# Node one-hots as the stationary operand, edge products of two groups in two halves of the array, and x in node order

## The chip, the cores and the metric

The kernel runs on one core of a Trainium2 chip. The metric is the device time of one execution in microseconds. The engines are PE (TensorE, matmul), DVE (VectorE), ACT (ScalarE), POOL (GpSimd) and SP (SyncE, which here only starts transfers); each works through its own list of instructions in order and waits on semaphores for the others.

## The reference

A graph network layer over 3125 nodes of 128 features and 53125 edges (sorted by destination, with self loops), each edge with 64 features of its own:

```
h   = relu(bn1(concat(x[src], edge_attr) @ W1 + b1))     # 53125 x 128
agg = segment_sum(h, dst) / max(count(dst), 1)           # 3125 x 128
h2  = relu(bn2(concat(x, agg) @ W2 + b2))                # 3125 x 256
z   = relu(h2 @ Wl + bl)
out = layernorm(x + z)
```

`bn` normalises each column over all rows, so bn1 needs the sum and the sum of squares of every column over all edges before any edge can be normalised.

## The kernel before

**Stages.** The product of x with the upper 128 rows of W1 is made once for each node, as a table `ytab` in DRAM, so that an edge needs one row of the table plus the product of its 64 features with the lower 64 rows of W1. The edge stage (to about 466 us) makes h for all edges, keeps it in SBUF (each fourth group goes to DRAM) and sums h and its square. A second pass (475 to 570 us) normalises, and sums h over windows of destinations; the node stage follows it. The change touches the edge stage alone, and the loads ahead of it.

**The edge stage.** There are 26 cycles (`NI`); a cycle i has four groups q = 0 to 3 (`U`), a group has four tiles of 128 edges, so 512 edges. I write (i, q) for a group. For each group:

- POOL gathers the table rows, one indirect transfer for each tile of 128 edges (`gather`, L672 to L688). The gathers of a group wait until h of the group four before it is ready (L676).
- PE multiplies the edge features with W1 (`product`, L762): an instruction takes two tiles, whose features stand in partitions 0 to 63 and 64 to 127, against a block-diagonal `w1e` of 128 x 256. The result is in PSUM bank `psP[q]`, one bank for each q.
- DVE adds the two (`make_h`, L1282) and counts up `h_ready`; adds h to a running sum (`sum_h`, L1335); ACT squares h (`squares`, L1019), and DVE adds the square to another running sum (`sum_sq`, L1342), one group late: `sum_sq` of (i, q-1) stands behind `sum_h` of (i, q).

**Rows that PE fetches.** In cycles 2 to 22 (`NODES`) one group (`NODEQ`, q = 2) has its first two tiles (even i) or three tiles (odd i) not gathered but made on PE (`node_tiles`, L55). DVE compares the source number of each edge with the node numbers (`node_onehots`, L1300), five batches for a cycle, each for 5 of 25 node tiles, in a ring of three buffers (`RING`). PE multiplies the table, kept in SBUF as three bfloat16 parts (`exact`), with the one-hots (`node_batch`, L774): the table part is stationary, the one-hots move, 256 or 384 columns at a time, 75 matmuls in a cycle. The result stands in `noderows` (feature by edge) and has to be turned: ACT copies it to SBUF (`rows_out`, L1097), and PE multiplies it with the identity into `psP[2]` (`rows_back`, L793).

**The counts and the product of x.** Once in a cycle DVE makes one-hots of the destinations (`onehots`, L1271), PE sums them (`counts`, L834) and ACT copies four rows of the result (`place_counts`, L1041). In 14 cycles PE also makes a piece of x @ W2 for the node stage (`x_product`, L845), reading the turned x of the table stage with a stride; ACT copies it (`x_product_out`, L1031) and saves it. `counts` and `x_product` share a PSUM bank and take turns through `cnt_placed` and `x_out`.

**Orders.** PE's order in a cycle is `edge_step` at L852: node batches 0 and 1, `x_product`, product (i, 2), node batch 2, product (i, 3), node batches 3 and 4, product (i+1, 0), `counts`, product (i, 1), `rows_back`. DVE's is `edge_step` at L1354: per group `make_h`, `sum_h`, `sum_sq`, and behind (i, 0) node one-hots 0 and 1 of the next cycle, behind (i, 1) the destinations' one-hots and node one-hots 2, behind (i, 2) node one-hots 3 and 4. ACT's is the loop at L1106: `rows_out`, the square of (i, 0), the store of the one-hots, `place_counts` (which waits for `counts` of the same cycle), the square of (i, 1), then `x_product_out` (for i below 14), then `node_numbers` of cycle i+2 (L1071), then the squares of (i, 2) and (i, 3). SP's is the loop at L526: store the fourth group, load edge features three cycles ahead, load source numbers.

Of the kernel before, what the change touches and what calls it, by code (L numbers as in the profile page):

```python
# [33 lines left out]
P = 128  # L34
# [4 lines left out]
U = 4  # L39
# [8 lines left out]
NODEQ = 2  # L48
# [6 lines left out]
def node_tiles(i):  # L55

    return 2 + i % 2 if ROWS0 <= i < ROWS1 else 0


def gnn_kernel(nc, E, x, xt, src, src_rows, dst, dst_rows, ea, W1, b1, g1, be1, W2, b2, g2, be2, Wl, bl, out):  # L60
# [29 lines left out]
    with ctx:  # L90
# [6 lines left out]
        def sem(name):  # L97
            return ctx.enter_context(nc.semaphore(name))
# [25 lines left out]
        w1e = sb("w1e", [P, 2, F])  # L124
        iota = sb("iota", [P, WIN])
        nodeid = sb("nodeid", [P, NT])[:, :]
        rowst_sb = sb("node_rows_turned", [P, MOST * P])
# [86 lines left out]
        XSTEPS = [(h, k, min(XP, PN - k)) for k in range(0, PN, XP) for h in range(H2)]  # L214
        w2x = agg[:, 0:H2 * P]
# [8 lines left out]
        assert XW <= 512 and len(XSTEPS) <= XT0 // (KEEP * GF) - 1  # L224
# [10 lines left out]
        noderows = psP[1][:, 0:MOST * P]  # L235
# [12 lines left out]
        PRODUCTS = [(0, q) for q in range(U)] + [(1, 0)]  # L248
        for i in range(1, NI):
            order = [(i, 1), (i, 2), (i, 3)] + ([(i + 1, 0)] if i + 1 < NI else [])  # L250
            PRODUCTS += order if i not in NODES else order[1:] + order[:1]

        def products_through(i, q):

            return PRODUCTS.index((i, q)) + 1

# [9 lines left out]
        s_w = sem("w_loaded")  # L266
# [12 lines left out]
        rows_kept = sem("node_rows_turned_copied")  # L279
        rows_added = sem("node_rows_added")  # L280
# [12 lines left out]
        s_tab = sem("table_written")  # L293
        x_ps = sem("w2_x_psum")
# [177 lines left out]
        def _(sp):  # L472
# [6 lines left out]
            sp.wait_ge(s_w, 1)  # L479
            sp.dma_start(w1e[0:FE, 0, :], W1[F:F + FE, :]).then_inc(s_cols, 16)  # L480
            sp.dma_start(w1e[FE:P, 1, :], W1[F:F + FE, :]).then_inc(s_cols, 16)
# [40 lines left out]

            load_ea(1, 1)
            load_nodes_of(ROWS0)
            load_ea(2, 0)
            for i in range(NI - 3):  # L526
                spill_out(i, i % 2)
                load_ea(i + 3, (i + 1) % 2)
                if i + 3 in NODES:
                    load_nodes_of(i + 3)  # L530
            spill_out(NI - 3, 1)
# [115 lines left out]
        def _(pool):  # L647
# [24 lines left out]
            def gather(i, q):  # L672

                g = U * i + q
                if g >= U:
                    pool.wait_ge(h_ready, g - 3)  # L676
                if i >= 2 and q == KEEP:
                    pool.wait_ge(spilled[i % 2], 16 * (i // 2))
                if (i + 1) * KEEP * GF > XT0 and q == 0:
                    pool.wait_ge(x_ps, len(XSTEPS))  # L680
# [54 lines left out]
        def _(pe):  # L735
# [26 lines left out]
            def product(i, par, nth, q):  # L762
                g = U * i + q
                if q == 0:
                    pe.wait_ge(ea_loaded[par], 16 * nth)
                pe.wait_ge(h_ready, g - U + 1)
                more = q == NODEQ and i in NODES
                for b in range(2):
                    last = pe.matmul(psP[q][:, b * 2 * F:(b + 1) * 2 * F], ea_cols(par, q, b),  # L769
                                     w1e[:, :, :].rearrange("p a f -> p (a f)"), start=(b == 0 or not more),  # L770
                                     stop=not more)
                last.then_inc(prod_ready, 1)

            def node_batch(i, b):  # L774

                t0, t1 = NODECUT[b]
                w = node_tiles(i) * P
                if (i, b) == (ROWS0, 0):
                    pe.wait_ge(consts_kept, 2)
                    pe.wait_ge(second_parts, len(PIECES))  # L780
                    pe.wait_ge(third_parts, len(PIECES))
                if b == 0:
                    pe.wait_ge(h_ready, U * (i - 1) + 2)
                pe.wait_ge(nhot_ready, batch_index(i, b) + 1)
                hots = node_chunks(i, b)
                for t in range(t0, t1):
                    for k in range(PARTS):
                        last = pe.matmul(noderows[:, 0:w], exact[k][0:PN, t * F:(t + 1) * F],  # L788
                                         hots[:, (t - t0) * w:(t - t0 + 1) * w], start=(t == 0 and k == 0),
                                         stop=(t == NT - 1 and k == PARTS - 1))  # L790
                last.then_inc(nhot_used, 1)

            def rows_back(i):  # L793

                pe.wait_ge(rows_kept, i - ROWS0 + 1)
                for j in range(node_tiles(i)):
                    last = pe.matmul(psP[NODEQ][:, j * F:(j + 1) * F], rowst_sb[:, j * P:(j + 1) * P], ident[:, :],
                                     start=False, stop=(j == node_tiles(i) - 1))
                last.then_inc(rows_added, 1)

            def ea_cols(par, q, b):

                at = (q * 2 + b) * P
                return eat[par][:, at:at + P]
# [12 lines left out]
            def product_first(q):  # L817
# [6 lines left out]
                for b in range(2):  # L824
                    last = pe.matmul(psP[q][:, b * 2 * F:(b + 1) * 2 * F], ea_cols(0, q, b),
                                     w1e[:, :, :].rearrange("p a f -> p (a f)"), start=(b == 0), stop=(q >= EARLY and b == 1))
# [18 lines left out]
            def x_product(m):  # L845

                h, k, n = XSTEPS[m]
                pe.wait_ge(cnt_placed, m + 1)
                pe.matmul(psT[1][:, 0:n * NT].rearrange("o (p t) -> o p t", t=NT), w2x[:, h * P:(h + 1) * P],  # L849
                          xtv[:, :, k:k + n].rearrange("f t p -> f p t"), start=True, stop=True).then_inc(x_ps, 1)  # L850

            def edge_step(i, par, nth):  # L852
                node = i in NODES
                if node:
                    node_batch(i, 0)
                    node_batch(i, 1)
                else:
                    product(i, par, nth, 1)
                if i <= len(XSTEPS):
                    x_product(i - 1)  # L860
                product(i, par, nth, 2)
                if node:
                    node_batch(i, 2)
                product(i, par, nth, 3)
                if node:
                    node_batch(i, 3)
                    node_batch(i, 4)
                if i + 1 < NI:
                    product(i + 1, 1 - par, (i + 1) // 2 + 1, 0)
                counts(i, par)  # L870
                if node:
                    pe.wait_ge(rows_kept, i - ROWS0 + 1)
                    product(i, par, nth, 1)
                    rows_back(i)
# [7 lines left out]
            product(1, 1, 1, 0)  # L882
# [119 lines left out]
        def _(act):  # L1002
# [94 lines left out]
            def rows_out(i):  # L1097

                w = node_tiles(i) * P
                act.wait_ge(nhot_used, NB5 * (i - ROWS0 + 1))  # L1100
                if i > ROWS0:
                    act.wait_ge(rows_added, i - ROWS0)
                act.activation(rowst_sb[:, 0:w], noderows[:, 0:w], ACT.Copy).then_inc(rows_kept, 1)  # L1103

            x_product_out(0)
            for i in range(1, NI - 1):  # L1106
                if i in NODES:
                    rows_out(i)
# [111 lines left out]
        def _(dve):  # L1220
# [8 lines left out]
            dve.memset(w1e[:, :, :], 0.0).then_inc(s_w, 1)  # L1229
# [15 lines left out]
            for a in range(2):  # L1245
                last = dve.tensor_tensor(w1e[:, a, :], w1e[:, a, :], sgn, ALU.mult)
            last.then_inc(s_wsgn, 1)
# [34 lines left out]
            def make_h(i, par, nth, q):  # L1282
# [9 lines left out]
                if q == NODEQ and i in NODES:  # L1292
                    w = node_tiles(i) * F
                    dve.wait_ge(rows_added, i - ROWS0 + 1)
# [59 lines left out]
            def edge_step(i, par, nth):  # L1354
                for q in range(U):
# [11 lines left out]
                    if q == 0:  # L1367
                        node_onehots(i + 1, 0)
                        node_onehots(i + 1, 1)
                    if q == 1:  # L1370
                        onehots(i + 1)
                        node_onehots(i + 1, 2)
                    if q == 2:
                        node_onehots(i + 1, 3)
                        node_onehots(i + 1, 4)
# [253 lines left out]
```

## Time and profile before

| | |
|---|---|
| median of 3 runs | 611.88 us (611.45 to 613.88) |
| profiled execution | 613.19 us, span of its instructions 611.4 us |
| busy in the span | PE 523.2 us (86%), PE weight loads 402.0, DVE 453.0 (74%), ACT 212.9, POOL 387.9 (63%) |
| mean granted PE clock | 0.934 of 2.4 GHz |
| edge stage, last gather begins | 465.51 us |
| second pass | 475 to 570 us |

The busy time of POOL counts the writing of a gather's descriptors and not the gap to the next one. Matmuls are pipelined: a record lasts longer than the spacing of two records, and the time of "xN" records in one row includes the last one's tail. A float32 matmul shows as two records, each with a weight load.

### The profile page before, as it was taken

What the parts mean: (1) busy time and instruction counts of PE and PEld (TensorE: products, weight loads), DVE (VectorE), ACT (ScalarE), POOL (GpSimd) and SP (SyncE); (2) the same over time, 40 slices, a digit from 0 to 9 for tenths busy, and PEclk for the clock granted to TensorE, in tenths of its full rate; (3) what the DMA queues carried; (4) which work ended last, traced back from release to release, by engine and by line L of the source; (5) the groups of instructions that cost most, each with busy time, mean ns of one, the idle gap of its engine ahead of it and who ended that gap; (6) DMA issues with size and microseconds to landing.
All of it is one profiled execution on the core that took longest, in us unless ns stands there. A gap on an engine that the chain in (4) does not pass through costs nothing.

```text
span 611.4 us, 11185 instructions
## 1 busy us (share of the span) xinstructions
PE 523.2 (86%) x3396; PEld 402.0 (66%) x3396; DVE 453.0 (74%) x747; ACT 212.9 (35%) x568; POOL 387.9 (63%) x487
## 2 busy tenths in 40 slices
PE   4639999999999999999897989854448999999983
PEld 4527666766757677777666676632225999999573
DVE  4598878686888868797877788654435877777786
ACT  2253222232313232222222221221116456666466
POOL 4777777777777777777777777777773233333500
PEclk9778999999999999999999999975568899999998
DMA  7635434443435444444444243442232478777004
GB/s 193 229 112 172 144 119 145 149 152 106 152 125 153 147 142 133 134 130 134 130 129 139 86 140 107 126 129 94 86 103 87 131 229 229 232 233 220 13 1 105
DMA packets 49561, 84.38 MB, mean 138 GB/s; under 512 B 11490, under 2 KB 25682, under 8 KB 49521
## 3 DMA queue, kind: packets, MB, share of 16 engines
q1 hardware_dynamic: 31420, 49.21, 25.3%
q0 software_dynamic: 11648, 23.88, 15.0%
q10 hardware_dynamic: 6453, 10.79, 5.1%
q8 instruction: 21, 0.34, 0.2%
q14 instruction: 19, 0.16, 0.1%
HBM read 63.74 MB, written 20.08 MB: 137 GB/s over the span
## 4 chain that ended last, share of the span: by engine, by line
POOL 41%; PE 27%; issue 17%; DVE 8%; DMA 4%; ACT 2%; ACTq 0%; POOLq 0%; DVEq 0%
POOL res L685 29%; POOL work L685 11%; PE psH L929 8%; PE psC L929 8%; PE psH L788 5%; DMA res<-ytab,srci 1%; PE psT L849 1%; DVE res L1481 1%; POOL res L667 1%; DMA srci<-in_src 1%; PE psH L769 1%; DMA res<-in_x,srci 1%; DVE res L1312 1%; ACT res L1068 1%; PE psT L769 1%
## 5 line engine op out<-in xcount | busy, mean ns | idle before, releaser
L685 POOL DMA_INDIRECT res<-ytab,srci x248 | 237.3, 957 | 75.6 <-issue 73.1
L788 PE MATMUL psH<-res 125*128 125x256 bf16 (+1 forms) x1575 | 222.5, 298 | 9.6 <-DVE res L1298 8.6
L788 PEld LDWEIGHTS psH<-res 125*128 125x128 bf16 x1575 | 152.3, 98 | 72.9 <-DVE res L1298 13.4
L685 POOL DMA_INDIRECT work<-ytab,srci x104 | 98.3, 946 | 31.7 <-issue 31.4
L1312 DVE TENSOR_TENSOR res<-agg,psC 125x1280 bf16<-125x1280 bf16 (+1 forms) x105 | 99.1, 971 | 4.9 <-PE psH L788 4.8
L1298 DVE TENSOR_TENSOR res<-psH,res 128x512 f32<-128x512 f32 x50 | 34.5, 689 | 80.3 <-DMA res<-ytab,srci 42.1
L1449 DVE TENSOR_TENSOR work<-res,psX 128x512 f32<-128x512 f32 x103 | 69.7, 687 | 21.0 <-PE psC L929 15.8
L710 POOL TENSOR_TENSOR agg<-agg,srci 128x64 f32 x104 | 32.3, 311 | 72.0 <-ACT srci L1163 58.5
L1345 DVE TENSOR_TENSOR psX<-agg,psX 128x512 f32<-128x512 f32 x103 | 71.1, 690 | 2.5 <-ACT agg L1023 2.4
L769 PE MATMUL psH<-w1e,work 128*128 128x256 f32 x200 | 55.6, 403 | 11.7 <-DVE res L1298 11.7
L1023 ACT ACTIVATE agg<-res 128x512 f32<-128x512 f32 x78 | 48.7, 624 | 46.7 <-DVE res L1298 28.8
L1338 DVE TENSOR_TENSOR psS<-res,psS 128x512 f32<-128x512 f32 x78 | 54.3, 696 | 2.7
L929 PE MATMUL psH<-work 128*128 128x128 f32 (+1 forms) x416 | 51.7, 278 | 1.0 <-DVE work L1449 1.0
L929 PE MATMUL psC<-work 128*128 128x128 f32 (+1 forms) x416 | 51.4, 277 | 0.0
L929 PEld LDWEIGHTS psH<-work 128*128 128x128 f32 x416 | 49.4, 195 | 1.2 <-DVE work L1449 1.2
L929 PEld LDWEIGHTS psC<-work 128*128 128x128 f32 x416 | 49.3, 195 | 0.0
L769 PEld LDWEIGHTS psH<-w1e,work 128*128 128x128 f32 x200 | 36.7, 201 | 18.8 <-issue 10.0
L1103 ACT ACTIVATE node_rows_turned<-psH 128x256 f32<-128x256 f32 (+1 forms) x21 | 9.1, 435 | 102.2 <-PE psH L788 102.2
L769 PEld LDWEIGHTS psT<-w1e,work 128*128 128x128 f32 x100 | 20.7, 216 | 32.4 <-issue 13.6
L769 PE MATMUL psC<-w1e,work 128*128 128x256 f32 x100 | 30.4, 431 | 11.6 <-DVE work L1298 11.6
L769 PE MATMUL psT<-w1e,work 128*128 128x256 f32 x100 | 30.4, 431 | 9.7 <-DVE res L1298 5.9
L1051 ACT ACTIVATE cnt<-psT 1x64 f32 x104 | 22.5, 216 | 36.4 <-PE psT L841 33.1
(204 smaller groups left out, 549.8 us busy)
## 6 DMA issues: line engine op xcount, KB each, us to landing
work<-in_edge_attr SPq DMA_DIRECT2D x26, 512.0 KB, 3.6
spill<-work SPq DMA_DIRECT2D x26, 256.0 KB, 2.4
res<-spill SPq DMA_DIRECT2D x25, 256.0 KB, 3.2
res<-ytab,srci POOLq DMA_INDIRECT x248, 2.5
hot_dram<-hotb ACTq DMA_DIRECT2D x13, 256.0 KB
hot_dram<-work ACTq DMA_DIRECT2D x13, 256.0 KB
hotb<-hot_dram SPq DMA_DIRECT2D x13, 256.0 KB, 2.7
work<-hot_dram SPq DMA_DIRECT2D x13, 256.0 KB, 2.9
```

What stands on the lines that cost most here:

```text
L685: pool.indirect_dma_start(rows[:, j * F:(j + 1) * F], None, ytab, bass.IndirectOffsetOnAxis(ap=srci[:, j, g:g + 1], axis=0)).then_inc(gath ...
L710: pool.tensor_tensor(w, w, wsum[:, q, :], ALU.add).then_inc(agg_added, 1)
L769: last = pe.matmul(psP[q][:, b * 2 * F:(b + 1) * 2 * F], ea_cols(par, q, b), w1e[:, :, :].rearrange("p a f -> p (a f)"), start=(b == 0 or ...
L788: last = pe.matmul(noderows[:, 0:w], exact[k][0:PN, t * F:(t + 1) * F], hots[:, (t - t0) * w:(t - t0 + 1) * w], start=(t == 0 and k == 0), ...
L929: last = pe.matmul(psA[q][:, 0:n], mx[:, q, j * F:(j + 1) * F], hotf[:, q, j * WIN:j * WIN + n], start=(j == 0), stop=(j == TILES - 1))
L1023: act.activation(sq[g % 2], slot(i, i % 2, q), ACT.Square).then_inc(sq_ready, 1)
L1051: last = act.activation(cnt[r:r + 1, bass.ds(bases[q], WIN)], psT[1][r:r + 1, q * WIN:(q + 1) * WIN], ACT.Copy)
L1298: dve.tensor_tensor(h, psP[q][:, :], h, ALU.add).then_inc(h_ready, 1)
L1312: dve.tensor_tensor(node_chunks(i, b).rearrange("p (t e two) -> p t e two", t=t1 - t0, two=2), srcz[i % 2][0:PN, 0:w].rearrange("p (e two) ...
L1338: last = dve.tensor_tensor(psS[:, :], slot(i, par, q), psS[:, :], ALU.add)
L1345: last = dve.tensor_tensor(psX[:, :], sq[g % 2], psX[:, :], ALU.add)
L1449: dve.tensor_tensor(tiles(mx[:, q, :]), tiles(hin), negu, ALU.max).then_inc(m_ready, 1)
```

## The change

- `NODEQ` is 3, and PE makes three tiles in each of cycles 2 to 22 (63 tiles; before 52).
- In `node_batch` the one-hots are stationary (128 edges) and the table parts move (128 columns): 3 x 25 x 3 = 225 matmuls of 128 columns in a cycle, which add directly into `psP[3]` on top of the edge product. `rows_out`, `rows_back`, `noderows` and their semaphores go.
- The edge products run in pairs of groups (`two_products`): even groups have their features in partitions 0 to 63, odd ones in 64 to 127, and matmuls of 64 rows by 128 columns alternate between the two halves. `w1e` is 128 x 128 (the same weights twice), and the features are laid out accordingly. A pair waits for h of its second bank's last user, and `make_h` of either group waits for both.
- `x_product` reads x from a transposed input in node order, loaded by SP in 7 chunks, two products to a chunk.
- PE's and DVE's orders change; ACT's order is as before, without `rows_out`.

```
 NODEQ = 3;  node_tiles(i): 3 in cycles 2 to 22
             def ea_product(par, q, j, start, stop):
                 half = slice(q % 2 * FE, (q % 2 + 1) * FE)
                 at = (q // 2 * TILES + j) * P
                 return pe.matmul(psP[q][:, j * F:(j + 1) * F], eat[par][half, at:at + P], w1e[half, :], start=start,
                                  stop=stop)
             def two_products(i, par, nth, q):
                 if q == 0:
                     pe.wait_ge(ea_loaded[par], 16 * nth)
                 pe.wait_ge(h_ready, U * (i - 1) + q + 2)
                 for j in range(TILES):
                     for k in (q, q + 1):
                         ...
                         last = ea_product(par, k, j, j == 0 or not more, not more)
# node_batch
                 for t in range(t0, t1):
-                    for k in range(PARTS):
-                        last = pe.matmul(noderows[:, 0:w], exact[k][0:PN, t * F:(t + 1) * F],
-                                         hots[:, (t - t0) * w:(t - t0 + 1) * w], ...)
+                    for j in range(node_tiles(i)):
+                        at = (t - t0) * w + j * P
+                        for k in range(PARTS):
+                            last = pe.matmul(psP[NODEQ][:, j * F:(j + 1) * F], hots[:, at:at + P],
+                                             exact[k][0:PN, t * F:(t + 1) * F], start=False, ...)
# x_product
                 pe.wait_ge(cnt_placed, m + 1)
+                pe.wait_ge(x_chunk, 16 * (m // H2 + 1))
-                pe.matmul(psT[1][...], w2x[:, h * P:(h + 1) * P], xtv[:, :, k:k + n].rearrange("f t p -> f p t"), ...)
+                pe.matmul(psT[1][:, 0:n * NT], w2x[:, h * P:(h + 1) * P], xchunk[:, 0:n * NT], start=True, stop=True)
# PE, one cycle
             def edge_step(i, par, nth):
+                two_products(i, par, nth, 2)
                 if node:
                     node_batch(i, 0)
                     node_batch(i, 1)
-                else:
-                    product(i, par, nth, 1)
                 if i <= len(XSTEPS):
                     x_product(i - 1)
-                product(i, par, nth, 2) ... product(i, par, nth, 3) ...
                 if node:
+                    for b in range(2, NB5):
+                        node_batch(i, b)
                 if i + 1 < NI:
+                    two_products(i + 1, 1 - par, (i + 1) // 2 + 1, 0)
                 counts(i, par)
-                if node: ... product(i, par, nth, 1); rows_back(i)
# DVE, make_h of the group that PE fetches
-                    dve.wait_ge(rows_added, i - ROWS0 + 1)
+                    dve.wait_ge(nhot_used, NB5 * (i - ROWS0 + 1))
# DVE, behind make_h, sum_h, sum_sq of group q of cycle i
                     if q == 0:
+                        node_onehots(i, 3)
+                    if q == 1:
+                        node_onehots(i, 4)
+                        onehots(i + 1)
+                    if q == 2:
                         node_onehots(i + 1, 0)
                         node_onehots(i + 1, 1)
+                    if q == 3:
+                        node_onehots(i + 1, 2)
# SP, in the loop of a cycle
+                if i % 2 and i // 2 + 1 < len(XCHUNKS):
+                    load_x_chunk(i // 2 + 1)        # waits for x_ps, then 128 x 500 float32
# ACT
             for i in range(1, NI - 1):
-                if i in NODES:
-                    rows_out(i)
                 squares(i, 0)
                 hot_out(i, i % 2)
                 place_counts(i)
                 squares(i, 1)
                 ...
```

## Rows read from the trace of the kernel before

**Rows 1.** The chain that ended last, by line (share of the span).

```profile
by line: POOL res L685 29.1%; issue 16.7%; POOL work L685 10.8%; PE psH L929 7.8%; PE psC L929 7.7%; PE psH L788 4.7%; DMA res<-ytab,srci 1.3%; PE psT L849 1.3%; DVE res L1481 1.1%; POOL res L667 1.1%; DMA srci<-in_src 1.0%; PE psH L769 1.0
```

**Rows 2.** One stretch: length; busy PE, PEld, DVE, ACT, POOL; PEclk; DMA share; GB/s.

```profile
105.00:404.00 299.00, 282.12 (x1794) 202.10 (x1792) 236.64 (x337) 79.33 (x189) 226.16 (x240) 1.00 0.44 132
```

**Rows 3.** Timeline of POOL: start, length, what, idle before.

```profile
421.77 0.94 POOL L685 DMA_INDIRECT work<-ytab,srci  x1 [0.30 <-issue]
...
465.51 0.94 POOL L685 DMA_INDIRECT work<-ytab,srci  x1 [0.30 <-issue]
```

**Rows 4.** Timeline of PE: node batches, product, counts and rows_back.

```profile
260.91 3.44 PE L788 MATMUL psH<-res 125*128 125x256 bf16 x30
...
266.35 0.61 PE L797 MATMUL psT<-ident,node_rows_turned 128*128 128x128 f32 x4
...
276.49 5.04 PE L788 MATMUL psH<-res 125*128 125x384 bf16 x30
281.37 1.03 PE L769 MATMUL psH<-w1e,work 128*128 128x256 f32 x4
282.23 0.60 PE L841 MATMUL psT<-work,onesb 128*128 128x256 bf16 x4
...
283.54 0.83 PE L797 MATMUL psT<-ident,node_rows_turned 128*128 128x128 f32 x6
```

**Rows 5.** Groups by form: busy us, mean ns of one, idle before.

```profile
L788 PEld LDWEIGHTS psH<-res 125*128 125x128 bf16 x1575 | 152.3, 98 | 72.9 <-DVE res L1298 13.4
...
L1312 DVE TENSOR_TENSOR res<-agg,psC 125x1920 bf16<-125x1920 bf16 x50 | 55.6, 1146 | 0.0
...
L849 PE MATMUL psT<-res,agg 128*128 128x500 f32 x24 | 24.7, 1119 | 10.0 <-ACT cnt L1051 10.0
```

**Rows 6.** Timeline of DVE: the fetched group of three tiles, sums, node one-hots.

```profile
255.76 0.28 DVE L1295 TENSOR_TENSOR res<-psT,res 128x128 f32<-128x128 f32 x1
255.96 0.54 DVE L1296 COPY res<-psT 128x384 f32<-128x384 f32 x1
...
272.06 0.69 DVE L1345 TENSOR_TENSOR psX<-agg,psX 128x512 f32<-128x512 f32 x1
272.66 2.21 DVE L1312 TENSOR_TENSOR res<-agg,psC 125x1920 bf16<-125x1920 bf16 x2
...
278.35 0.69 DVE L1298 TENSOR_TENSOR res<-psH,res 128x512 f32<-128x512 f32 x1 [1.55 <-DMA res<-ytab,srci]
...
280.28 1.54 DVE L1312 TENSOR_TENSOR res<-agg,psC 125x1280 bf16<-125x1280 bf16 x2
```

**Rows 7.** Timeline of ACT: the copies of the counts and the square behind them.

```profile
266.50 0.90 ACT L1051 ACTIVATE cnt<-psT 1x64 f32 x4 [1.22 <-PE psT L841]
267.43 0.63 ACT L1023 ACTIVATE agg<-res 128x512 f32<-128x512 f32 x1
```

**Rows 8.** Timelines of DVE, PE and ACT around the product of x in cycle 2.

```profile
54.27 2.04 PE L849 MATMUL psT<-res,agg 128*128 128x500 f32 x2
...
55.92 0.69 DVE L1298 TENSOR_TENSOR work<-psC,work 128x512 f32<-128x512 f32 x1 [0.62 <-DMA work<-ytab,srci]
...
56.35 0.59 ACT L1037 ACTIVATE agg<-psT 128x500 f32<-128x500 f32 x1 [3.52 <-PE psT L849]
...
58.53 0.69 DVE L1345 TENSOR_TENSOR psX<-agg,psX 128x512 f32<-128x512 f32 x1 [1.19 <-ACT agg L1023]
```

**Rows 9.** Timeline of PE behind two idle times, and the granted clock of the first.

```profile
44.45 2.22 PE L849 MATMUL psT<-res,agg 128*128 128x500 f32 x2 [9.99 <-ACT cnt L1051]
...
48.17 1.69 PE L769 MATMUL psC<-w1e,work 128*128 128x256 f32 x4
49.70 1.03 PE L769 MATMUL psH<-w1e,work 128*128 128x256 f32 x4
...
404.74 2.07 PE L769 MATMUL psT<-w1e,work 128*128 128x256 f32 x4 [2.20 <-DVE res L1296]
...
40.00:49.00 9.00, 4.55 (x8) 2.79 (x9) 8.74 (x16) 4.86 (x11) 6.82 (x7) 0.50 0.41 132
```

More of the change, by code:

```diff
@@ L47 @@
 ROWS1 = 23
-NODEQ = 2
+NODEQ = 3
 MOST = 3
@@ L55, in node_tiles, with gnn_kernel @@
 def node_tiles(i):
-    return 2 + i % 2 if ROWS0 <= i < ROWS1 else 0
-def gnn_kernel(nc, E, x, xt, src, src_rows, dst, dst_rows, ea, W1, b1, g1, be1, W2, b2, g2, be2, Wl, bl, out):
+    if not ROWS0 <= i < ROWS1:
+        return 0
+    return 3
+def gnn_kernel(nc, E, x, xt, xcols, src, src_rows, dst, dst_rows, ea, W1, b1, g1, be1, W2, b2, g2, be2, Wl, bl, out):
     N, F = x.shape
@@ L214, in gnn_kernel @@
         XSTEPS = [(h, k, min(XP, PN - k)) for k in range(0, PN, XP) for h in range(H2)]
+        XCHUNKS = [(k, n) for h, k, n in XSTEPS if h == 0]
         w2x = agg[:, 0:H2 * P]
@@ L223, in gnn_kernel @@
         assert SQ0 >= NAGG // 2 and SQ0 + 2 * GF <= NAGG - MOST * P
-        assert XW <= 512 and len(XSTEPS) <= XT0 // (KEEP * GF) - 1
+        xchunk = agg[:, SQ0 - GF:SQ0 - GF + XW]
+        assert Z0 + MOST * P <= SQ0 - GF
+        assert XW <= 512
         psT = [pb(f"psT{i}", [P, 512]) for i in range(2)]
@@ L246, in node_chunks @@
             return ring[batch_index(i, b) % RING][0:PN, 0:(t1 - t0) * node_tiles(i) * P]
[L248 to L251, printed above, removed]
+        PRODUCTS = [(0, q) for q in range(U)] + [(i, q) for i in range(1, NI) for q in range(U)]
         def products_through(i, q):
-            return PRODUCTS.index((i, q)) + 1
+            return PRODUCTS.index((i, q | 1 if i else q)) + 1
         negu = psX[:, 0:F].unsqueeze(1).broadcast_to([P, TILES, F])
@@ L265, in gnn_kernel @@
         s_w1x = sem("w1x_loaded")
-        s_w = sem("w_loaded")
         s_rows = sem("dst_loaded")
@@ L293, in gnn_kernel @@
         s_tab = sem("table_written")
+        x_chunk = sem("x_chunk_loaded")
         x_ps = sem("w2_x_psum")
@@ L478, in _ @@
                              ).then_inc(s_x[k], 16)
-            sp.wait_ge(s_w, 1)
-            sp.dma_start(w1e[0:FE, 0, :], W1[F:F + FE, :]).then_inc(s_cols, 16)
-            sp.dma_start(w1e[FE:P, 1, :], W1[F:F + FE, :]).then_inc(s_cols, 16)
+            for a in range(2):
+                sp.dma_start(w1e[a * FE:(a + 1) * FE, :], W1[F:F + FE, :]).then_inc(s_cols, 16)
             sp.dma_start(w2x, W2[0:F, :]).then_inc(s_cols, 16)
@@ L521, in load_nodes_of, with load_x_chunk @@
                              ).then_inc(s_srcb, 16)
+            def load_x_chunk(m):
+                k, n = XCHUNKS[m]
+                if m == 0:
+                    sp.wait_ge(prod_ready, EARLY)
+                else:
+                    sp.wait_ge(x_ps, H2 * m)
+                sp.dma_start(xchunk[:, 0:n * NT], xcols[:, k * NT:(k + n) * NT]).then_inc(x_chunk, 16)
             load_ea(1, 1)
             load_nodes_of(ROWS0)
+            load_x_chunk(0)
             load_ea(2, 0)
@@ L530, in _ @@
                     load_nodes_of(i + 3)
+                if i % 2 and i // 2 + 1 < len(XCHUNKS):
+                    load_x_chunk(i // 2 + 1)
             spill_out(NI - 3, 1)
@@ L760, in _ @@
             pe.wait_ge(s_wsgn, 2)
-            def product(i, par, nth, q):
-                g = U * i + q
+            def ea_product(par, q, j, start, stop):
[4 more added lines that the diff above has]
+            def two_products(i, par, nth, q):
                 if q == 0:
                     pe.wait_ge(ea_loaded[par], 16 * nth)
[L766 to L772, printed above, removed]
+                pe.wait_ge(h_ready, U * (i - 1) + q + 2)
+                for j in range(TILES):
+                    for k in (q, q + 1):
+                        more = k == NODEQ and i in NODES
+                        last = ea_product(par, k, j, j == 0 or not more, not more)
+                        if j == TILES - 1:
+                            last.then_inc(prod_ready, 1)
             def node_batch(i, b):
@@ L786, in node_batch @@
                 for t in range(t0, t1):
[L787 to L790, printed above, removed]
-                last.then_inc(nhot_used, 1)
[L793 to L804, printed above, removed]
+                    for j in range(node_tiles(i)):
+                        at = (t - t0) * w + j * P
+                        for k in range(PARTS):
+                            last = pe.matmul(psP[NODEQ][:, j * F:(j + 1) * F], hots[:, at:at + P],
+                                             exact[k][0:PN, t * F:(t + 1) * F], start=False,
+                                             stop=(t == NT - 1 and j == node_tiles(i) - 1 and k == PARTS - 1))
+                last.then_inc(nhot_used, 1)
             def turn_first(q):
@@ L823, in product_first @@
                     pe.wait_ge(s_idx, 1)
-                for b in range(2):
-                    last = pe.matmul(psP[q][:, b * 2 * F:(b + 1) * 2 * F], ea_cols(0, q, b),
-                                     w1e[:, :, :].rearrange("p a f -> p (a f)"), start=(b == 0), stop=(q >= EARLY and b == 1))
+                for j in range(TILES):
+                    last = ea_product(0, q, j, j == 0, q >= EARLY and j == TILES - 1)
                 if q < EARLY:
@@ L848, in x_product @@
                 pe.wait_ge(cnt_placed, m + 1)
-                pe.matmul(psT[1][:, 0:n * NT].rearrange("o (p t) -> o p t", t=NT), w2x[:, h * P:(h + 1) * P],
-                          xtv[:, :, k:k + n].rearrange("f t p -> f p t"), start=True, stop=True).then_inc(x_ps, 1)
+                pe.wait_ge(x_chunk, 16 * (m // H2 + 1))
+                pe.matmul(psT[1][:, 0:n * NT], w2x[:, h * P:(h + 1) * P], xchunk[:, 0:n * NT], start=True, stop=True
+                          ).then_inc(x_ps, 1)
             def edge_step(i, par, nth):
                 node = i in NODES
+                two_products(i, par, nth, 2)
                 if node:
@@ L856, in edge_step @@
                     node_batch(i, 1)
-                else:
-                    product(i, par, nth, 1)
                 if i <= len(XSTEPS):
                     x_product(i - 1)
-                product(i, par, nth, 2)
                 if node:
[L863 to L867, printed above, removed]
+                    for b in range(2, NB5):
+                        node_batch(i, b)
                 if i + 1 < NI:
-                    product(i + 1, 1 - par, (i + 1) // 2 + 1, 0)
+                    two_products(i + 1, 1 - par, (i + 1) // 2 + 1, 0)
                 counts(i, par)
[L871 to L874, printed above, removed]
             turn_first(0)
@@ L881, in _ @@
             counts(0, 0)
-            product(1, 1, 1, 0)
+            two_products(1, 1, 1, 0)
             for i in range(1, NI):
@@ L1227, in link @@
                 dve.wait_ge(s_dv, chain[0])
-            dve.memset(w1e[:, :, :], 0.0).then_inc(s_w, 1)
             dve.memset(cnt[:, :], 0.0)
@@ L1244, in _ @@
             dve.wait_ge(s_cols, 16 * 6)
-            for a in range(2):
-                last = dve.tensor_tensor(w1e[:, a, :], w1e[:, a, :], sgn, ALU.mult)
-            last.then_inc(s_wsgn, 1)
+            dve.tensor_tensor(w1e[:, :], w1e[:, :], sgn, ALU.mult).then_inc(s_wsgn, 1)
             link(dve.tensor_scalar(c(C_AG), c(C_G), 0.0, 2.0, ALU.is_ge, ALU.mult))
@@ L1367, in edge_step @@
                     if q == 0:
+                        node_onehots(i, 3)
+                    if q == 1:
+                        node_onehots(i, 4)
+                        onehots(i + 1)
+                    if q == 2:
                         node_onehots(i + 1, 0)
                         node_onehots(i + 1, 1)
-                    if q == 1:
-                        onehots(i + 1)
+                    if q == 3:
                         node_onehots(i + 1, 2)
-                    if q == 2:
-                        node_onehots(i + 1, 3)
-                        node_onehots(i + 1, 4)
             def keep_in_psum():
@@ L1611 @@
         'x_turned': x.reshape(N // NT, NT, F).transpose(2, 1, 0),
+        'x_columns': x.T,
         'src': src.reshape(NG, P, TILES).transpose(1, 2, 0),
```

22 lines of the change are left out of this document (3 added, 19 removed).

## The prediction

> **What bounds the kernel now.** I read the chain of waits first: its largest parts are POOL's gathers, 29.1 and 10.8% of the span, with the gaps between them ("issue", 16.7%) [rows 1]. The timeline of POOL then shows these gathers back to back, 0.94 us each with a 0.30 us gap, so 1.25 us apart, up to the one at 465.51 [rows 3]; the second pass begins when h of its group is done. From 105 to 404 us PE is busy for 282 of 299 us at full clock, DVE for 237 [rows 2]. So POOL sets the pace, 13 or 14 gathers (16.3 or 17.5 us) a cycle in cycles 2 to 22, and PE follows closely. This works because PE runs ahead: its node batches of cycle i+1 go to a bank of their own while DVE is still at groups 1 to 3 of cycle i. The orders by which that holds are what I followed next.
>
> **The change, part by part.**
>
> *Gathers.* PE takes 63 tiles for 52, so 11 gathers fall away: 11 x 1.25 = 13.8 us less on POOL. This is a gain only where POOL still sets the pace, at 13 gathers, 16.3 us a cycle.
>
> *Node batches.* 225 matmuls of 128 columns take the place of 75 of 256 or 384. Thirty of these took 3.44 us at 256 columns and 5.04 at 384 [rows 4], so 128 columns cost 1.60 / 30 = 53 ns; thirty at 128 would take 1.84 us with the last one's tail, 61 ns. I take 55: 225 x 0.055 = 12.4 us a cycle, 2.5 a batch. Weight loads, now one for every 128 columns, must hide in that: the load records last 98 ns [rows 5], and a load of this shape did fit every 109 ns beside a 256-column matmul, so the bounds are 53 and 109. I choose the low end because a float32 pair, whose load has twice the bytes, runs at (0.83 - 0.61) / 2 = 110 ns [rows 4], the time of two passes of 128 columns, so there too the load hides. The other end is a rival below.
>
> *Edge products.* A pair of groups is 8 matmuls, 16 records of 128 columns. One after the other, at the 110 ns above, that is 1.76 us; with the two halves side by side, half, 0.88. I take 1.3, two pairs a cycle. Before, four products of about 0.87 us (0.86 from one start to the next [rows 4]) took 3.5, and rows_back 0.6 to 0.8: these go. The Trainium skill ("TensorEngine Tiling (Array Packing)", Key Properties) says that a change of the tiling mode drains the array, which happens four times a cycle here. No run here shows it; by the tail of a record it would be about 0.2 us each, an estimate, 0.8 x 21 = 17 us more.
>
> *Product of x.* The strided read made 500 columns cost 2.04 us for two records [rows 8], 1119 ns on average each [rows 5]; a 256-column product has four records in 1.03 us, so 500 contiguous columns cost about 0.84. The seven loads stand on SP's queue; each waits for products already due and lands most of a cycle before its use, and the stores and loads behind it have as long. Nothing for it; if a load came late it would be PE's wait in one cycle of two, a few us in all. At the start, one memset, one wait of SP and one multiply go, off the gathers' path: within 0.3 us.
>
> *Counts and orders: where a new wait closes.* PE now adds the node batches straight into the bank of group (i, 3), and its first pair of the next cycle waits for h of (i, 3). DVE makes that h behind sum_sq of (i, 1) and two node one-hots. That sum_sq needs ACT's square of (i, 1), which ACT still does behind the copies of the counts, and `counts` is the last thing in PE's cycle. So these are in series in each cycle, and PE stands idle from `counts` until h of (i, 3) is made. Before, the same sum_sq stood there too, but PE was by then in the next cycle's batches. The loop, from one first pair to the next:
> - PE: pair 1.3, five batches 12.4, pair 1.3, counts 0.60 [rows 4]: 15.6
> - ACT: four copies 0.90 and the square 0.63 [rows 7], with hand-overs 1.7
> - DVE: sum_sq 0.60 to the next start, two one-hot batches 2.2, then the fetched group's two instructions, 255.76 to 256.50, 0.75 [rows 6], and a hand-over: 3.6
>
> 20.9 us against POOL's 16.3. PE is idle 5.3 of them.
>
> A second wait closes in cycles 2 to 14. ACT does the square of (i, 2) behind the copy of the product of x, which PE makes in cycle i+1 behind batch 1; DVE makes node one-hots 2 of cycle i+1 behind the sum of that square; PE's batch 2 needs them. In cycle 2 of before, 2.22 us passed from the end of the product (56.31) to that sum (58.53), which was waiting for ACT even then [rows 8]. Now the product (0.84 + 0.2 tail) + 2.2 + sum 0.6 + one-hots 1.15 [rows 5] stand between batches 1 and 2: 5.0 us. Batches 3 and 4 then each wait about 0.5 more, since DVE needs 1.93 (278.35 to 280.28 [rows 6]) + 1.07 for each one-hot batch, PE 2.5. So 6.0 more: 26.9 us.
>
> *The clock.* Idle PE loses its clock. After 9.99 us of idle it was granted 0.50 (1.2 GHz), a product took 1.69 us for 1.03, and full clock was back by 49.70, 5.25 us after it began again; 2.20 us of idle before 404.74 were enough (2.07 for 1.03) [rows 9]. Both new waits are longer. About 5 us at half clock lose 2.5 us for the first gap; for the second net 1.5, as the slower batch 2 hides the 0.5s behind it.
>
> *Sum.* Cycle 2's first pair starts when h of (1, 3) is there, 55.92 + 0.69 = 56.6 [rows 8]. Thirteen cycles at 26.9 and eight at 20.9, less 2 for the two short products of x: 515. Clock: 21 x 2.5 + 13 x 1.5 = 72. So h of (22, 3) comes at 56.6 + 587 = 643.6. The gathers of (23, 3) wait for just that, where before they began at 421.77 [rows 3]; cycles 23 to 25 have no node batches and run at POOL's pace, as does all behind them as before. The end shifts by 643.6 - 421.8 = 222 us, from the profiled 613.2 to 835; on the median of 611.9, which is 1.3 below that execution, 834.
>
> **The rivals.**
> - *The clock holds.* The same loops without 72 us: 762. For it: PE is 75% busy in such a cycle; against: each idle time of 2 us and more that I read was followed by half clock [rows 9].
> - *Loads do not hide at 128 columns.* By the load's 98 ns [rows 5] a cycle gets 225 x 43 ns = 9.7 us more, 21 x 9.7 = 203, so up to 1037, less where the clock is low anyway. Against it is the float32 pair above. The Trainium skill ("TensorE: Matmul & The Clock Gate", Back-to-back issue gap) gives about 81 ns for a load and matmul of 128 columns in a real kernel. By that figure, as an estimate, it would be 225 x 26 ns x 21 = 123 more, 957; no row here has such a pair in bfloat16.
> - *PE stays at 1.2 GHz through cycles 2 to 22*, because work with these gaps never regains it: batches 24.8 and pairs 5.2, 15 us a cycle for the 2.5 to 4 counted, so about 1080. Against: it came back after 5 us of steady work at 49.70.
> - *On the other side: POOL remains the bound.* PE's own 15.6 us fit in 16.3, so if DVE reaches h of (i, 3) without waiting for ACT, only the 11 gathers count: 598. It decides at a wait of 0.7 us between counts and that h; I find 5.3. For it is only that POOL may run a cycle ahead, some 10 us of slack, used up in two cycles.
> - *The halves do not run side by side* (the change doesn't do what it says): 2 x 0.46 x 21 = 19 more, 853, inside the forecast's own range.
>
> **How the numbers follow.** Forecast 0.66, clock holds 0.12, loads do not hide 0.13, clock never back 0.05, POOL bound 0.04. The forecast's own range is 795 to 885 (pairs 0.88 or with drains, 1.8 to 3 us a gap). I widen it to 755 for the held clock, and to 935 for loads that hide in part; that leaves out about 2 in 10. 0.5% is about what a measurement of this kernel can tell from no change (its runs lie within 0.4%). Faster 0.04, within it 0.01, slower 0.95.
>
> **What would show it.** Right: PE idle for about 5 us behind each `counts`, released by DVE's copy of the fetched group; the sum of squares waiting for ACT in each cycle; cycles near 31 us until about 460 and near 23 behind that; POOL idle, released by DVE; granted clock near 0.8 there. Wrong: POOL still 1.25 us apart throughout, or PE without a gap behind `counts`. Matmuls of node batches 55 ns apart at full clock would show the hidden loads, a pair of 0.9 us the two halves.

## The result and the profile after

The changed kernel takes 834.55 us (median of 4 runs, 833.39 to 834.92) against 612.75 for the kernel before in the same comparison: ratio 1.3618, interval 1.3581 to 1.3654. The forecast was 834. The profiled execution took 834.87 us, its span is 833.1 us.

The page: busy time of the engines, PE's granted clock in 40 slices of the span, and the chain by line.

```profile
PE 596.5 (72%) x6858; PEld 551.8 (66%) x6858; DVE 471.4 (57%) x745; ACT 205.4 (25%) x547; POOL 376.6 (45%) x476
...
PEclk9759688687787787787778899988897559999998
...
PE psC L802 39%; DVE res L1291 7%; PE psH L921 6%; PE psC L921 6%; PE psT L773 5%; POOL res L692 4%; PE psH L773 3%; ACT agg L1015 3%; PE psT L841 1%; ACT cnt L1043 1%; PE psT L850 1%; POOL work L692 1%; DVE work L1275 1%; ACT agg L1072 1%; ACT agg L1029 1%
```

POOL led the chain before [rows 1]; now PE's node batches do (L802), with DVE's one-hots, its copy of the fetched group and ACT's squares and copies between them: a loop through three engines. POOL's own busy time even fell. PE's idle time is in the list of waits (who waited for whom: us in total, times, longest):

```profile
PE psT L773 <- DVE work L1275: 108.0, 21, 5.2
PE psC L802 <- DVE res L1291: 52.3, 13, 4.1
```

The first is the first pair of cycles 3 to 23 waiting for h of the fetched group, 21 times, up to 5.2 us; the second is batch 2 of cycles 2 to 14 waiting for its one-hots, 13 times, up to 4.1 us. The timeline of PE shows both in cycle 3, and the first alone in cycle 17 (start, length, what, idle before; a row of 0.58 us is the first of a pair's 16 records):

```profile
85.49 0.58 PE L773 MATMUL psT<-w1e,work 64*128 64x128 f32 x1 [5.24 <-DVE work L1275]
85.49 0.58 PE L773 MATMUL psC<-w1e,work 64*128 64x128 f32 x1
...
87.50 6.62 PE L802 MATMUL psC<-res 125*128 125x128 bf16 x90
93.95 1.06 PE L850 MATMUL psT<-agg 128*128 128x500 f32 x2
99.08 10.11 PE L802 MATMUL psC<-res 125*128 125x128 bf16 x135 [4.08 <-DVE res L1291]
109.12 1.16 PE L773 MATMUL psH<-w1e,work 64*128 64x128 f32 x16
110.22 0.61 PE L841 MATMUL psT<-work,onesb 128*128 128x256 bf16 x4
116.07 0.58 PE L773 MATMUL psT<-w1e,work 64*128 64x128 f32 x1 [5.24 <-DVE work L1275]
...
497.47 0.58 PE L773 MATMUL psT<-w1e,work 64*128 64x128 f32 x1 [5.24 <-DVE work L1275]
...
499.48 14.64 PE L802 MATMUL psC<-res 125*128 125x128 bf16 x225
514.05 1.16 PE L773 MATMUL psH<-w1e,work 64*128 64x128 f32 x16
515.14 0.61 PE L841 MATMUL psT<-work,onesb 128*128 128x256 bf16 x4
521.00 0.58 PE L773 MATMUL psT<-w1e,work 64*128 64x128 f32 x1 [5.24 <-DVE work L1275]
```

A cycle is 30.6 us there (85.49 to 116.07) and 23.5 here (497.47 to 521.00). Both halves of a pair start at the same time (85.49). The first pair takes 2.0 us (85.49 to 87.50), the second, at full clock, 1.16 with its tail: PE comes back from each wait at half clock, 1.2 GHz, and later has full clock again. Two stretches show it (length; busy PE, PEld, DVE, ACT, POOL; granted clock, the number behind POOL's; DMA share; GB/s):

```profile
85.49:87.50 2.01, 2.01 (x17) 1.79 (x17) 0.67 (x1) 0.00 (x0) 0.94 (x1) 0.50 0.55 181
505.00:515.00 10.00, 10.00 (x180) 9.90 (x177) 5.64 (x8) 0.00 (x0) 7.35 (x9) 1.00 0.22 60
```

The other two sides of the loop, in cycle 16. ACT first: the copies of the counts, which waited for PE, and the square behind them. Then DVE: the sum of that square, waiting for ACT; two one-hot batches; the two instructions that make h of the fetched group.

```profile
492.35 0.90 ACT L1043 ACTIVATE cnt<-psT 1x64 f32 x4 [14.49 <-PE psT L841]
493.27 0.63 ACT L1015 ACTIVATE agg<-res 128x512 f32<-128x512 f32 x1
```

```profile
493.93 0.69 DVE L1324 TENSOR_TENSOR psX<-agg,psX 128x512 f32<-128x512 f32 x1 [6.75 <-ACT agg L1015]
494.54 2.21 DVE L1291 TENSOR_TENSOR res<-agg,psC 125x1920 bf16<-125x1920 bf16 x2
496.66 0.28 DVE L1274 TENSOR_TENSOR work<-psC,work 128x128 f32<-128x128 f32 x1
496.87 0.55 DVE L1275 COPY work<-psC 128x384 f32<-128x384 f32 x1
```

Read downwards, 492.35 to 497.42 is one piece with no gap over 0.05 us, and PE starts at 497.47. It is the sum of [rows 6, 7], now in series.

Last, POOL, which the forecast had waiting for h of (22, 3) before the gathers of (23, 3):

```profile
613.26 0.94 POOL L692 DMA_INDIRECT work<-ytab,srci  x1 [5.39 <-DVE work L1275]
629.20 0.94 POOL L692 DMA_INDIRECT res<-ytab,srci  x1 [14.99 <-PE psC L802]
...
644.18 0.94 POOL L692 DMA_INDIRECT work<-ytab,srci  x1 [0.30 <-issue]
```

The gathers of (23, 3) do begin at 644.18 (643.6 was forecast), but not for that reason: see the points below.

### The profile page after: what moved, and what is told of

It is laid out like the page before. It is cut to its first block, busy times and chain, and to the rows that moved or that the text cites. A ratio compares the mean times of both kernels' runs of the same rounds, so it can differ in the third digit from the quotient of the medians.

```text
span 833.1 us, 18032 instructions
## 1 busy us (share of the span) xinstructions
PE 596.5 (72%) x6858; PEld 551.8 (66%) x6858; DVE 471.4 (57%) x745; ACT 205.4 (25%) x547; POOL 376.6 (45%) x476
## 4 chain that ended last, share of the span: by engine, by line
PE 64%; DVE 14%; ACT 7%; issue 6%; POOL 6%; DMA 2%; ACTq 1%; DVEq 0%; POOLq 0%
PE psC L802 39%; DVE res L1291 7%; PE psH L921 6%; PE psC L921 6%; PE psT L773 5%; POOL res L692 4%; PE psH L773 3%; ACT agg L1015 3%; PE psT L841 1%; ACT cnt L1043 1%; PE psT L850 1%; POOL work L692 1%; DVE work L1275 1%; ACT agg L1072 1%; ACT agg L1029 1%
## 5 line engine op out<-in xcount | busy, mean ns | idle before, releaser
L692 POOL DMA_INDIRECT res<-ytab,srci x300 | 285.9, 953 | 280.3 <-DVE res L1277 181.5
L802 PEld LDWEIGHTS psC<-res 125*128 125x128 bf16 x4725 | 323.4, 111 | 66.2 <-DVE res L1291 61.5
L802 PE MATMUL psC<-res 125*128 125x128 bf16 x4725 | 329.2, 243 | 52.3 <-DVE res L1291 52.3
L773 PE MATMUL psT<-w1e,work 64*128 64x128 f32 x208 | 52.8, 431 | 131.8 <-DVE work L1275 108.0
L773 PEld LDWEIGHTS psT<-w1e,work 64*128 64x128 f32 x208 | 45.3, 319 | 139.5 <-DVE work L1275 113.8
L1291 DVE TENSOR_TENSOR res<-agg,psC 125x1920 bf16<-125x1920 bf16 x105 | 118.8, 1148 | 14.3 <-PE psC L802 14.3
L692 POOL DMA_INDIRECT work<-ytab,srci x41 | 38.7, 943 | 60.2 <-DVE work L1275 53.8
L773 PE MATMUL psC<-w1e,work 64*128 64x128 f32 x208 | 52.9, 431 | 0.0
L773 PE MATMUL psH<-w1e,work 64*128 64x128 f32 x416 | 35.2, 306 | 14.8 <-DVE res L1277 14.8
L773 PEld LDWEIGHTS psC<-w1e,work 64*128 64x128 f32 x208 | 45.3, 319 | 0.1
```

The lines of the kernel that those rows point to most:

```text
L692: pool.indirect_dma_start(rows[:, j * F:(j + 1) * F], None, ytab, bass.IndirectOffsetOnAxis(ap=srci[:, j, g:g + 1], axis=0)).then_inc(gath ...
L773: return pe.matmul(psP[q][:, j * F:(j + 1) * F], eat[par][half, at:at + P], w1e[half, :], start=start, stop=stop)
L802: last = pe.matmul(psP[NODEQ][:, j * F:(j + 1) * F], hots[:, at:at + P], exact[k][0:PN, t * F:(t + 1) * F], start=False, stop=(t == NT - 1 ...
L1291: dve.tensor_tensor(node_chunks(i, b).rearrange("p (t e two) -> p t e two", t=t1 - t0, two=2), srcz[i % 2][0:PN, 0:w].rearrange("p (e two) ...
```

## The experiments

The theory was that all of the loss is in waits that PE's and DVE's new orders make out of ACT's old one, and in the clock lost in them. The main rival was that PE's new work is the bound: three times the matmuls, each with a weight load, and products by halves. The first four ran beside one set of runs of the kernel before, the last four beside another.

**Both waits away.**

```
             for i in range(1, NI - 1):
                 squares(i, 0)
                 hot_out(i, i % 2)
-                place_counts(i)
                 squares(i, 1)
+                squares(i, 2)
+                place_counts(i)
+                squares(i, 3)
                 if i < len(XSTEPS):
                     x_product_out(i)
                 if i + 2 in NODES:
                     node_numbers(i + 2)
-                for q in (2, 3):
-                    squares(i, q)
```

> Only ACT's order differs from the changed kernel: the squares of groups 1 and 2 stand ahead of the copies of the counts, that of group 3 ahead of the copy of the product of x. Theory (the loss is the two waits through ACT, and the clock lost in them): both waits go, PE has some 15 us of work in a cycle (16 with a product of x) against POOL's 13 gathers x 1.25 = 16.3, so POOL is the bound again with 11 gathers fewer: about 600 us, clock near 1 until 404. Rival (PE's own new work, 225 matmuls of 128 columns with a weight load each and the products by halves, is the bound): no gain, about 830, at least above 750.

Measured: 609.52 us, ratio to the kernel before 0.9931 (0.9908 to 0.9954). Moving three of ACT's squares ahead takes 225 us away, and the rival falls: the same 6858 matmuls, the same halves, and no loss. But 9 us of the expected gain are missing. In PE's timeline a cycle with a product of x takes 17.1 us (162.95 to 180.06 between first batches), over POOL's 16.3, and DVE waits for ACT 12 times, 31.7 us in all, one of them here:

```profile
162.95 5.20 PE L802 MATMUL psC<-res 125*128 125x128 bf16 x90
167.99 1.06 PE L850 MATMUL psT<-agg 128*128 128x500 f32 x2
168.88 7.70 PE L802 MATMUL psC<-res 125*128 125x128 bf16 x135
176.51 1.16 PE L773 MATMUL psH<-w1e,work 64*128 64x128 f32 x16
177.61 0.61 PE L841 MATMUL psT<-hotb,onesb 128*128 128x256 bf16 x4
178.97 0.37 PE L773 MATMUL psT<-w1e,work 64*128 64x128 f32 x1 [0.75 <-DVE work L1275]
180.06 5.20 PE L802 MATMUL psC<-res 125*128 125x128 bf16 x90
```

```profile
188.42 0.69 DVE L1324 TENSOR_TENSOR psX<-agg,psX 128x512 f32<-128x512 f32 x1 [2.81 <-ACT agg L1015]
```

At full clock the node batches run at (7.70 - 0.22) / 134 = 56 ns a matmul.

**The first wait away, the second left.** The edit of the first experiment, but only `squares(i, 1)` goes ahead of `place_counts(i)`:

```
-                place_counts(i)
                 squares(i, 1)
+                place_counts(i)
```

> Of the changed kernel only the first wait is taken away: the square of group 1 stands ahead of the copies of the counts, all else as it was. Theory: no idle PE behind the counts; cycles 2 to 14 keep the 4 us wait behind batch 1 (about 22 us each with the clock it costs), cycles 15 to 22 run at POOL's 16.3: 56.6 + 13 x 22 + 8 x 16.3 = 473, some 8 to 12 more for the gathers of cycle 23, so about 670. Rival (PE's work is the bound): about 830.

Measured: 686.78 us, 1.1194 (1.1166 to 1.1222). The first wait alone was worth 834.55 - 686.78 = 148 us. The time is 17 us more than expected. About 14 of these are cycles 2 to 14, which take 23.1 us (the products of x at 155.63 and 178.71 are that far apart) and not 22: the 4.08 us gap is still there, and batches 2 to 4 behind it still begin at half clock (9.96 us for 7.70):

```profile
178.71 1.06 PE L850 MATMUL psT<-agg 128*128 128x500 f32 x2
183.84 9.96 PE L802 MATMUL psC<-res 125*128 125x128 bf16 x135 [4.08 <-DVE res L1291]
```

**The second wait away, the first left.** `squares` of groups 2 and 3 go ahead of `x_product_out`, `place_counts` stays first:

```
                 squares(i, 1)
+                squares(i, 2)
+                squares(i, 3)
                 if i < len(XSTEPS):
                     x_product_out(i)
                 ...
-                for q in (2, 3):
-                    squares(i, q)
```

> Of the changed kernel only the second wait is taken away: the squares of groups 2 and 3 stand ahead of the copy of the product of x, but the square of group 1 stays behind the copies of the counts. Theory: all cycles become like 15 to 22 (23 us, 24 with a product of x): 56.6 + 13 x 24 + 8 x 23 = 553, about 750 us in all, 83 less than the changed kernel. Rival (PE's work is the bound): about 830.

Measured: 748.15 us, 1.2195 (1.2159 to 1.2230): the second wait alone was worth 86 us. Its timeline has no idle time behind the product of x any more, and its list of waits keeps the first line of the changed kernel's to the digit:

```profile
182.34 1.06 PE L850 MATMUL psT<-agg 128*128 128x500 f32 x2
183.24 7.70 PE L802 MATMUL psC<-res 125*128 125x128 bf16 x135
```

```profile
PE psT L773 <- DVE work L1275: 108.0, 21, 5.2
```

148 + 86 = 234, near the 225 of both, where the third wait below and POOL's pace set a new floor.

**The clock's part.** PE is kept at work in the first wait; nothing else changes (the results go to a bank whose content is done with):

```
                 counts(i, par)
+                if node:
+                    pe.wait_ge(h_ready, U * i + 3)
+                    for _ in range(84):
+                        pe.matmul(psP[2][:, 0:P], onesb[:, :], onesb[:, :], start=True, stop=True)
```

> The changed kernel with 84 more matmuls of 128 columns behind the counts of each of cycles 2 to 22, whose result is overwritten unused: about 4.7 of the 5.2 us in which PE waited. Both waits stay. Theory (each wait also costs clock): what the first wait costs in clock goes, 2.6 us in cycles 2 to 14 (a first pair of 2.0 for 0.93 us, the first batch at 90 ns for 56) and 2.1 in 15 to 22: 51 us less, about 784. Rival (the waits cost only their own length): about 834, or some more since the new matmuls delay the next pair.

Measured: 779.60 us, 1.2686 (1.2638 to 1.2735): 55 us less than the changed kernel, for 21 x 4.7 us more of PE work. So the waits cost more than their length. In its timeline the filler ends 0.56 us ahead of the pair, the pair then takes 1.1 us (226.75 to 227.84) and not 2.0, and the first two batches 5.20 and not 6.62; behind the second wait, which stays, batches 2 to 4 still take 9.34:

```profile
200.37 5.20 PE L802 MATMUL psC<-res 125*128 125x128 bf16 x90
205.40 1.06 PE L850 MATMUL psT<-agg 128*128 128x500 f32 x2
210.53 9.34 PE L802 MATMUL psC<-res 125*128 125x128 bf16 x135 [4.08 <-DVE res L1295]
...
221.34 4.85 PE L870 MATMUL psT<-onesb 128*128 128x128 bf16 x84
226.75 0.37 PE L773 MATMUL psT<-w1e,work 64*128 64x128 f32 x1 [0.56 <-DVE work L1279]
...
227.84 4.36 PE L802 MATMUL psC<-res 125*128 125x128 bf16 x75
```

The mean granted clock rose from 0.79 (105 to 450 us of the changed kernel) to 0.94 (105 to 404 us here), and behind the filler it is full:

```profile
226.70:233.00 6.30, 6.25 (x107) 6.13 (x108) 0.70 (x1) 0.00 (x0) 0.95 (x1) 1.00 0.46 146
```

**A third wait, found in the first experiment.** The copy of the product of x, which waits for PE in the middle of the next cycle, moves behind the square of group 0 of that cycle:

```
             for i in range(1, NI - 1):
                 squares(i, 0)
+                if 1 <= i - 1 < len(XSTEPS):
+                    x_product_out(i - 1)
+                if i > ROWS0 - 1 and i + 1 in NODES:
+                    node_numbers(i + 1)
                 hot_out(i, i % 2)
                 squares(i, 1)
                 squares(i, 2)
                 place_counts(i)
                 squares(i, 3)
-                if i < len(XSTEPS):
-                    x_product_out(i)
-                if i + 2 in NODES:
-                    node_numbers(i + 2)
```

> As e1_squares_ahead, and ACT's copy of the product of x moves behind the square of group 0 of the next cycle, with the node numbers. In e1 PE's cycles with a product of x took 17.1 us, 0.75 of it idle until h of the fetched group, and DVE waited 2.8 us for that square behind the copy. Theory (what is left of the loss in e1 is a third wait through ACT's order): cycles of 16.4 us against POOL's 16.3, waits of POOL on h nearly gone, about 600 us. Rival (DVE, with three one-hot tiles in all cycles, is the bound in e1): no change from 609.

Measured (median of 5 runs): 601.50 us, 0.9813 (0.9797 to 0.9828). This beats both kernels, the kernel before by 1.9%. POOL is the bound again: from 105 us to its last gather it has one wait of more than its usual 0.3 us, of 3.9 us:

```profile
POOL res L692 <- DVE work L1275: 3.9, 1, 3.9
```

```profile
105.00:404.00 299.00, 290.66 (x4805) 274.88 (x4802) 260.28 (x349) 76.86 (x177) 223.36 (x237) 0.99 0.50 142
```

In the second fence (length, busy PE, PEld, DVE, ACT, POOL, clock) PE is busy 97% of that stretch and DVE 87%, at a clock of 0.99: 225 matmuls a cycle fit, with nothing to spare.

**The halves in turn.** On the version of the last experiment:

```
-                for j in range(TILES):
-                    for k in (q, q + 1):
+                for k in (q, q + 1):
+                    for j in range(TILES):
```

> As e7, but a pair of groups runs its four matmuls of the upper half first and then those of the lower. Theory (the halves run side by side only when they alternate): a pair takes 1.8 us and not 0.93, two pairs a cycle, PE's cycles 17.2 to 18.0 us against POOL's 16.3, so about 25 us more than e7, 625. Rival (order makes no difference): as e7.

Measured: 620.16 us, 1.0117 (1.0098 to 1.0136), 19 us more than the last. A pair takes 1.71 us with its tail for 1.16:

```profile
188.01 7.70 PE L802 MATMUL psC<-res 125*128 125x128 bf16 x135
195.64 1.71 PE L773 MATMUL psH<-w1e,work 64*128 64x128 f32 x16
197.28 0.61 PE L841 MATMUL psT<-work,onesb 128*128 128x256 bf16 x4
```

0.55 us more and not the 0.87 expected (1.8 for 0.93); the trace has the first records of the lower half beside the last ones of the upper, so a part still overlaps. PE is now busy in all 299 us from 105 to 404, so most of 2 x 0.55 x 21 = 23 us is seen.

**The product of x with a stride.** Also on that version; `x_product` reads `xtv` as in the kernel before, and the loads of `xchunk` go. POOL's wait for the last product, which guards the turned x in the kernel before, comes back with it.

```
-                pe.wait_ge(x_chunk, 16 * (m // H2 + 1))
-                pe.matmul(psT[1][:, 0:n * NT], w2x[:, h * P:(h + 1) * P], xchunk[:, 0:n * NT], ...)
+                pe.matmul(psT[1][:, 0:n * NT].rearrange("o (p t) -> o p t", t=NT), w2x[:, h * P:(h + 1) * P],
+                          xtv[:, :, k:k + n].rearrange("f t p -> f p t"), ...)
...
```

> As e7, but the product of x reads the turned x of the table stage with a stride, as the kernel before, and the seven loads go. Theory (x in node order is worth what the product gets shorter, 1.88 to 0.89 us, where PE is as long as POOL): cycles 2 to 12 take 17.4 us, about 11 us more than e7, 611. Rival (hidden behind POOL): as e7.

Measured: 609.34 us, 0.9944 (0.9922 to 0.9966), 8 us more than with x in node order. The product takes 2.07 us there and 1.06 here, both with the tail:

```profile
186.65 2.07 PE L848 MATMUL psT<-res,agg 128*128 128x500 f32 x2
```

**Three tiles in all cycles, in the kernel before.**

```
-    return 2 + i % 2 if ROWS0 <= i < ROWS1 else 0
+    return 3 if ROWS0 <= i < ROWS1 else 0
```

> The kernel before, with one change: three tiles in each of cycles 2 to 22, as the changed kernel has, one-hots still moving. 11 gathers fewer. Theory (PE has no room for it in that form): its cycles of three tiles take 17.3 us, 18.9 with a product of x, against POOL's 16.3, so the last node batch is done at about 430 for 397, past the 407 at which the first gather of cycle 23 could begin, and the end moves by some 20: about 633. Rival (POOL is the bound there too): 600.

Measured: 634.09 us, 1.0332 (1.0311 to 1.0353). With the one-hots moving, PE has no room for the third tile: it is busy for 297.0 of the 299 us from 105 to 404, a cycle with a product of x takes 18.9 us (180.98 to 199.90), and POOL waits for DVE 20 times at one group alone:

```profile
180.98 1.03 PE L769 MATMUL psH<-w1e,work 128*128 128x256 f32 x4
...
199.90 1.03 PE L769 MATMUL psH<-w1e,work 128*128 128x256 f32 x4
```

```profile
POOL work L685 <- DVE work L1298: 38.3, 20, 2.5
```

So the third tile in all cycles costs 21 us in the old form and fits in the new one, once the waits are gone (601.50). Of the parts of the change, alternating the halves was worth 19 us there and x in node order 8; the one-hots as the stationary operand were not tried apart.

## Why the prediction was right, point by point

- *The loop behind the counts.* Forecast 5.3 us of idle PE, measured 5.24 in 20 of 21 cycles and 3.12 in the last. Shown by the second experiment: undoing its cause takes 148 us away.
- *The wait between batches 1 and 2.* Forecast 5.0 us of which 1.0 is the product itself, measured 4.0 to 4.1 idle in 11 of 13 cycles and 3.76 behind the two short products. Shown by the third experiment, 86 us.
- *The clock.* Forecast 2.5 us a cycle for the first gap and 1.5 for the second, 72 in all. The filler gives 55 us back for the first gap alone, against 21 x 2.5 = 52. For the second gap, batches 2 to 4 take 9.34 to 10.16 us for 7.70, 1.6 to 2.5 more; the forecast had 1.5 for the clock and 1.0 for waits of batches 3 and 4, and the trace shows no such waits apart.
- *PE's work.* 55 ns a matmul was forecast, 56 measured: the loads hide. The rival of 98 ns falls with it, and so does the figure of 81 ns of the Trainium skill ("TensorE: Matmul & The Clock Gate", Back-to-back issue gap): by the trace it is too high for this kernel. For a pair I took the middle of 0.88 and 1.76, 1.3; at full clock it is 1.10 from its start to the next work (109.12 to 110.22), between the two and not the 0.9 that was named as the sign, but the halves do run side by side: 1.64 when they run in turn (195.64 to 197.28 in that run). The drain at a change of tiling mode that the Trainium skill names ("TensorEngine Tiling (Array Packing)", Key Properties) costs at most 0.1 us at the one change that I read: in the run with the filler the last records of a pair start 0.2 us ahead of the first batch, where the records of one half are 0.1 apart.
- *The sum was right by two errors that cancel, which is luck.* Cycles 2 to 21 were 7 us shorter than forecast (cycle 22 begins at 613.05; forecast 56.6 + 400 + 7 x 23.4 = 620), 2.0 of it in cycle 2 alone, which takes 28.9; in the others the second pair makes 0.2 a cycle. Cycle 22 makes no one-hots for a next one and is 20.0 us (to 633.05), 3.4 less. Against these 10 us stands a wait that I missed: the rows of cycle 23 lie where the one-hot ring was, so POOL's first gather of cycle 23 waits for the last node batch (L681 of the kernel before). It cost nothing there: that batch was done at 396.97, and the gather began at 406.78. Now it held POOL 14.99 us until 629.20, and twelve gathers that would have run in that time ran behind it: (23, 3) began at 644.18, where h of (22, 3) alone would have allowed about 633. So the step "the gathers of (23, 3) wait for just that" did not hold, and without the wait that I missed the kernel would have taken some 11 us less than forecast, an estimate from 644.18 - 633. From 644.18 on the forecast holds: the last gather begins 43.7 us later, as before (421.77 to 465.51). The trace shows this; it was not tried apart. In the version that beats both kernels the 3.9 us are at the same gather: it begins at 395.43, 0.96 us after the product behind the last node batch (394.47), as here 629.20 is 0.97 us after 628.23.
- *The rivals.* The clock neither held (0.50 behind the waits) nor stayed at 1.2 GHz (1.00 from 505 to 515 us). POOL as the bound came true only in the version without the three waits: 601.5, where 598 had been worked out.

## What to carry to other kernels

When a result starts to be added in place (here into the bank of the edge product) instead of in a bank of its own, the producer of the next round waits for the consumer of this one: follow what that consumer's instruction stands behind on its engine, and what that in turn waits for on the others, before counting any cycle. An order that was harmless while one engine ran ahead closes a loop when it no longer does; three squares moved ahead were worth 225 us. And add to a wait of PE what its clock costs behind it: here the filler alone gave back 55 us of clock on 108 us of idle time.

## What the runs showed of the hardware that was not expected

Even in turn, the two halves of the array overlap in part: a pair took 1.71 us with its tail, and 1.16 when the halves alternate, where 1.8 and 0.93 had been expected. And the change from 64-row float32 to full-height bfloat16 work behind a pair cost at most 0.1 us.
